# Where the turned probabilities, the late key sums and the hidden layer norm stand in a two-layer cross-attention kernel

## The reference

```python
x = single_head_attention(x, ctx)                       # softmax over 361 context rows
for layer in (1, 2):
    h = layer_norm(x) * scale + offset
    q = h @ wq + bq; k = ctx @ wk + bk; v = ctx @ wv + bv          # heads of 128
    k = concat(k, bias_k); v = concat(v, bias_v)                   # one more key and value
    x = x + softmax(q k^T / sqrt(128)) v @ wo + bo
x = x + gelu(layer_norm(x) @ w_fc1 + b_fc1) @ w_fc2 + b_fc2
```

## Time and profile before

| | |
|---|---|
| median of three runs | 1750.81 us (1749.13 to 1752.08) |
| the profiled execution, own time | 1752.08 us |
| its span in the profile | 1750.2 us |
| PE busy | 1728.7 us |
| DVE busy | 1194.3 us |
| ACT busy | 751.4 us |
| POOL busy | 870.7 us |
| DMA queue, share of 16 engines | 33.2% |

### The profile page before, as it was taken

The page is one execution under the profiler, slowest core; times in us unless marked ns, Lnnn a source line. Parts: engine busy times, 40 slices in busy tenths (PEclk is TensorE's granted clock), DMA queues, the critical chain, the costliest instruction groups (busy, mean ns, idle before and its releaser), DMA issues.

```text
span 1750.2 us, 30234 instructions
## 1 busy us (share of the span) xinstructions
PE 1728.7 (99%) x10854; PEld 1679.7 (96%) x10854; DVE 1194.3 (68%) x2718; ACT 751.4 (43%) x1624; POOL 870.7 (50%) x727
## 2 busy tenths in 40 slices
PE   8999999999999999999999999999999999999999
PEld 5899999999998999999999999999999999999999
DVE  3667676766877766667876666668776676677675
ACT  3635334334544333335453343345443333444654
POOL 2674252454484452534882523555834535336754
PEclk9999999999999999999999999999999999999999
DMA  7732332223452232324342322334423233204332
GB/s 277 253 114 79 78 98 53 71 82 96 138 158 63 78 83 72 89 48 144 115 126 73 86 48 75 85 106 131 144 52 89 63 75 86 79 19 140 132 129 80
DMA packets 162784, 175.09 MB, mean 100 GB/s; under 512 B 99660, under 2 KB 115276, under 8 KB 162636
## 3 DMA queue, kind: packets, MB, share of 16 engines
q1 hardware_dynamic: 159388, 168.86, 33.2%
q10 hardware_dynamic: 3248, 4.30, 0.8%
HBM read 150.67 MB, written 5.14 MB: 89 GB/s over the span
## 4 chain that ended last, share of the span: by engine, by line
PE 92%; DVE 5%; ACT 1%; issue 1%; DMA 1%; SPq 0%; ACTq 0%; DVEq 0%
PE psum L819 29%; PE psum L820 29%; PE psum L821 29%; PE psum L1157 2%; PE psum L853 2%; DVE key_stage_late L1710 1%; DVE pT L1684 1%; DVE prob L1989 1%; DVE centred L1890 0%; DMA key_stage_late<-head_w_dram 0%; SPq L563 0%; PE psum L832 0%; DVE a_lo L1684 0%; ACT prob L1520 0%; DVE stats L1980 0%
## 5 line engine op out<-in xcount | busy, mean ns | idle before, releaser
L653 POOL TENSOR_TENSOR wbuf_hi<-stage,zero_col 128x512 fp32r<-128x512 f32 x256 | 272.5, 1065 | 673.9 <-PE psum L821 497.1
L708 POOL TENSOR_TENSOR wbuf_lo<-stage,wbuf_hi 128x512 fp32r<-128x512 f32 x256 | 336.8, 1316 | 20.1
L819 PE MATMUL psum<-pT,ctx_rows_hi 128*128 128x250 f32 (+1 forms) x1152 | 331.4, 288 | 5.9 <-DVE pT L1684 5.7
L820 PE MATMUL psum<-pT,ctx_rows_hi 128*128 128x250 f32 (+1 forms) x1152 | 331.1, 287 | 0.0
L821 PE MATMUL psum<-pT,ctx_rows_lo 128*128 128x250 f32 (+1 forms) x1152 | 330.4, 287 | 0.0
L819 PE MATMUL psum<-ctxT_hi,a_hi 128*125 128x362 f32 (+1 forms) x832 | 277.8, 334 | 0.5
L821 PE MATMUL psum<-ctxT_hi,a_lo 128*125 128x362 f32 (+1 forms) x832 | 273.0, 328 | 0.0
L820 PE MATMUL psum<-ctxT_lo,a_hi 128*125 128x362 f32 (+1 forms) x832 | 272.8, 328 | 0.0
L819 PE MATMUL psum<-a_hi,wbuf_hi 128*128 128x400 f32 x720 | 252.7, 351 | 0.6 <-DVE xT L1905 0.6
L820 PE MATMUL psum<-a_lo,wbuf_hi 128*128 128x400 f32 x720 | 247.7, 344 | 0.0
L821 PE MATMUL psum<-a_hi,wbuf_lo 128*128 128x400 f32 x720 | 247.6, 344 | 0.0
(11 more groups left out here) (220 smaller groups left out, 3397.4 us busy)
## 6 DMA issues: line engine op xcount, KB each, us to landing
stage<-head_w_dram SPq DMA_DIRECT2D x256, 256.0 KB, 2.8
mlp_stage<-mlp_w_dram SPq DMA_DIRECT2D x32, 512.0 KB, 3.3
ctx_rows_in<-ctx_dram SPq DMA_DIRECT2D x20, 768.0 KB, 5.3
ctxT_in<-ctxT_dram SPq DMA_DIRECT2D x20, 724.0 KB, 5.4
p_b<-p_scratch SPq DMA_DIRECT2D x64, 200.0 KB, 3.6
sorted<-prob SPq DMA_DIRECT2D x256, 48.0 KB, 2.0
key_stage<-head_w_dram SPq DMA_DIRECT2D x22, 256.0 KB, 4.7
pT<-prob SPq DMA_DIRECT2D x96, 48.0 KB, 2.0
```

Source lines behind the costliest of these rows:

```text
L653: return nc.gpsimd.tensor_tensor(out, in_, zero_col[0:in_.shape[0], :].broadcast_to(tuple(in_.shape)), ALU.add)
L708: nc.gpsimd.tensor_tensor(lo, held, hi.bitcast(F32), ALU.subtract).then_inc(stage_free, 1)
L819: pe.matmul(out, a_h, x_hi, start=start, stop=False)
L820: pe.matmul(out, a_h, x_lo, start=False, stop=False)
```

## The change

Turning: `in_squares` keeps only the blocks with x = 0 (not the first two steps of units 2 and 4), with one held buffer. 16 blocks of a phase go in squares instead of 22, and 36 by PE instead of 30. The blocks that move are x = 1 of (1,1), (1,2), (2,2), (3,1), (3,2) and (4,2).

Late keys: all ten are in phase 0, two in each of the same five steps. The first ("a") stands ahead of `maxima(k, b, 1)` and the second ("b") at the end of the step. SP loads two behind each of the sorts of (0,1,0), (0,2,0), (0,3,0), and the others behind weights 8, 18, 20 and 21.

SP's reads of first rows: they stand behind all sorts of the same place, so those of heads 0 and 1 now stand behind the sort of (1, 1, 0).

DVE: an `o` piece at the head of place "a" (steps (1,3) and (3,3)) is added after `normalise` and not ahead of it. `hidden_centre` stands behind `normalise(k, b, 1)`, and the reciprocals of the variance are interleaved with `attended_lo`. In the single-head part two low parts of the context stand earlier.

PE: `hidden_mean` and `hidden_variance` stand behind `scores(k, b, 1)`. ACT: the four squares stand together behind `probs_hi(5, 1, 0)`. `PIECES`: v4 and v9 stand behind k7 and k12.

```diff
-    (2, 0, "b"): "q7 v2 v3 v4 o2 k7", ...
+    (2, 0, "b"): "q7 v2 v3 o2 k7 v4", ...
-    (4, 0, "b"): "q12 v7 v8 v9 o7 k12", ...
+    (4, 0, "b"): "q12 v7 v8 o7 k12 v9", ...
-LATE_KEYS_IN = 2
-LATE_KEYS_AT = [(0, 1), (0, 2), (0, 3), (1, 2), (1, 3)]
-FIRST_LATE_KEY_BEHIND = 9
-LATE_KEYS_BEHIND_SORTED = [(0, 2, 0), (0, 3, 0), (1, 0, 0), (1, 3, 0)]
+LATE_KEYS_AT = {(0, 1): "ab", (0, 2): "ab", (0, 3): "ab", (1, 2): "ab", (1, 3): "ab"}
+LATE_KEYS_BEHIND = {8: 1, 18: 1, 20: 1, 21: 1}
+LATE_KEYS_BEHIND_SORTED = {(0, 1, 0): 2, (0, 2, 0): 2, (0, 3, 0): 2}
 def in_squares(k, b, x):
-    return 0 < k + (x == 0) and k < len(UNITS) - 1 and not (k in LATE and b < 2) and not (x == 1 and b in (0, NB - 1))
-HELD = 2
+    return k < len(UNITS) - 1 and x == 0 and not (k in LATE and b < 2)
+HELD = 1
@@ SP
-                    reads = [h for h in VALUES if P0_READ_AT[h] == i and UNIT_OF[h] < LAST_UNIT]
                     for at in IN_SQUARES:
                         if SORTED_AT[at] == i:
-                            while reads and T_AT[LAST_BLOCK_OF[reads[0]]] < T_AT[at]:
-                                load_first_probs(ph, reads.pop(0))
                             sort_squares(ph, *at)
-                            if ph < LATE_KEYS_IN and at in LATE_KEYS_BEHIND_SORTED:
+                            for _ in range(LATE_KEYS_BEHIND_SORTED.get(at, 0) if ph == 0 else 0):
                                 load_late_key_weights(next(keys))
-                    for h in reads:
-                        load_first_probs(ph, h)
+                    for h in VALUES:
+                        if P0_READ_AT[h] == i and UNIT_OF[h] < LAST_UNIT:
+                            load_first_probs(ph, h)
@@ PE
                         scores(k, b, 0)
-                        if (k, b) == MEAN_IN:
-                            hidden_mean()
 ...
+                        scores(k, b, 1)
                         if (k, b) == VARIANCE_IN:
                             hidden_variance()
-                        scores(k, b, 1)
+                        if (k, b) == MEAN_IN:
+                            hidden_mean()
@@ ACT
-                        if STEPS[STEPS.index((k, b)) + 1:][:1] == [MEAN_IN]:
-                            hidden_square(ph, part)
 ...
                         probs_hi(k, b, 0)
+                        if (k, b) == MEAN_IN:
+                            hidden_squares(ph)
@@ DVE
-                        added_first = 1 if in_squares(k, b, 0) and pieces((k, b, "a"))[:1] and pieces((k, b, "a"))[0][0] == "o" else 0
-                        run_pieces((k, b, "a"), 0, added_first)
                         normalise(k, b, 0)
-                        run_pieces((k, b, "a"), added_first)
+                        run_pieces((k, b, "a"))
 ...
+                        if ph == 0 and "a" in LATE_KEYS_AT.get((k, b), ""):
+                            late_key_sums(next(keys))
                         maxima(k, b, 1)
+                        normalise(k, b, 1)
                         if (k, b) == MEAN_IN:
                             hidden_centre(ph)
                         if (k, b) == VARIANCE_IN:
-                            hidden_invert(ph, 0, DC - 1)
-                        normalise(k, b, 1)
-                        if before is not None:
+                            for part in range(DC - 1):
+                                attended_lo(*before, part, part + 1)
+                                hidden_invert(ph, part, part + 1)
+                            attended_lo(*before, DC - 1, DC)
+                        elif before is not None:
                             attended_lo(*before)
```

More of the change, by code:

```diff
@@ L90 @@
 KEYS = 7
-LATE_KEYS_IN = 2
-LATE_KEYS_AT = [(0, 1), (0, 2), (0, 3), (1, 2), (1, 3)]
-FIRST_LATE_KEY_BEHIND = 9
-LATE_KEYS_BEHIND_SORTED = [(0, 2, 0), (0, 3, 0), (1, 0, 0), (1, 3, 0)]
-KEYS_BEFORE = LAYERS * H - LATE_KEYS_IN * len(LATE_KEYS_AT)
+LATE_KEYS_AT = {(0, 1): "ab", (0, 2): "ab", (0, 3): "ab", (1, 2): "ab", (1, 3): "ab"}
+LATE_KEYS_BEHIND = {8: 1, 18: 1, 20: 1, 21: 1}
+LATE_KEYS_BEHIND_SORTED = {(0, 1, 0): 2, (0, 2, 0): 2, (0, 3, 0): 2}
+KEYS_BEFORE = LAYERS * H - len("".join(LATE_KEYS_AT.values()))
 PHASES = [(half, l) for l in range(LAYERS) for half in range(HALVES)]
@@ L427, in in_columns @@
             return ap.rearrange("p t (a j) -> p t a j", j=SQUARE)
-        held = [sorted0[:, :, :]] + [pT[:, 0:GROUPS, WIDE - RUN:WIDE].bitcast(F32)]
+        held = [sorted0[:, :, :]]
         def held_chunks(j):
@@ L558, in sort_squares @@
                     sp.wait_ge(p0_sent[x], 32 * n)
-                if x == 1:
-                    wait(sp, u_mm, ph * U_LAYER)
                 for a in range(GROUPS):
@@ L589, in _ @@
                 for i in range(early + 2 * (ph > 0), W_AT["v", H - 1]):
-                    reads = [h for h in VALUES if P0_READ_AT[h] == i and UNIT_OF[h] < LAST_UNIT]
                     for at in IN_SQUARES:
                         if SORTED_AT[at] == i:
-                            while reads and T_AT[LAST_BLOCK_OF[reads[0]]] < T_AT[at]:
-                                load_first_probs(ph, reads.pop(0))
                             sort_squares(ph, *at)
-                            if ph < LATE_KEYS_IN and at in LATE_KEYS_BEHIND_SORTED:
+                            for _ in range(LATE_KEYS_BEHIND_SORTED.get(at, 0) if ph == 0 else 0):
                                 load_late_key_weights(next(keys))
-                    for h in reads:
-                        load_first_probs(ph, h)
+                    for h in VALUES:
+                        if P0_READ_AT[h] == i and UNIT_OF[h] < LAST_UNIT:
+                            load_first_probs(ph, h)
                     load_weights(ph, i)
-                    if ph < LATE_KEYS_IN and i == FIRST_LATE_KEY_BEHIND:
-                        load_late_key_weights(next(keys))
+                    if ph == 0:
+                        for _ in range(LATE_KEYS_BEHIND.get(i, 0)):
+                            load_late_key_weights(next(keys))
                     if i == X_BEHIND:
@@ L1431, in norm_hi, with hidden_squares @@
                                              bias=norm_p[:, PARAMETERS[j], c, OFFSET_COL:OFFSET_COL + 1]).then_inc(n_hi, 1)
-            def hidden_square(ph, c):
-                act.wait_ge(hn_cen, ph * DC + c + 1)
-                nc.scalar.activation(x_held[:, c, :], centred[:, c, :], ACT.Square).then_inc(hn_sq, 1)
+            def hidden_squares(ph):
+                for c in range(DC):
+                    act.wait_ge(hn_cen, ph * DC + c + 1)
+                    nc.scalar.activation(x_held[:, c, :], centred[:, c, :], ACT.Square).then_inc(hn_sq, 1)
             def hidden_roots(ph):
@@ L1482, in queries_hi @@
                 def queries_hi(h):
-                    if ph < LATE_KEYS_IN and h == ASIDE[0]:
-                        act.wait_ge(kw_sum, KEYS_BEFORE + (ph + 1) * len(LATE_KEYS_AT))
+                    if ph == 0 and h == ASIDE[0]:
+                        act.wait_ge(kw_sum, LAYERS * H)
                     nc.scalar.activation(made_queries(h)[0], made("q", h), ACT.Identity, bias=bias_of(BQ, h))\
@@ L1801, in single_head @@
                 turned_lo(0)
+                ctx_columns_lo(1, 0)
                 queries1_lo(1)
@@ L1805, in single_head @@
                 probs0_lo(2)
-                ctx_columns_lo(1, 0)
+                ctx_columns_lo(1, 1)
                 queries1_lo(2)
@@ L1811, in single_head @@
                 probs0_lo(3)
-                ctx_columns_lo(1, 1)
                 queries1_lo(3)
@@ L1964, in add_output, with run_pieces @@
                         add(columns(xT[:, m, :]), made("o", h, m), columns(xT[:, m, :]), l, m, h == 0).then_inc(y_done, 1)
-                def run_pieces(place, start=0, stop=None):
-                    for kind, h in pieces(place)[start:stop]:
+                def run_pieces(place):
+                    for kind, h in pieces(place):
                         {"q": queries_lo, "k": through_keys_lo, "v": values_lo, "o": add_output}[kind](h)
@@ L2088, in layer @@
                             hidden_scale(ph, 0, 1)
-                    if ph < LATE_KEYS_IN and (k, b) in LATE_KEYS_AT:
+                    if ph == 0 and "b" in LATE_KEYS_AT.get((k, b), ""):
                         late_key_sums(next(keys))
-                    if ph == LATE_KEYS_IN - 1 and (k, b) == (3, 2):
+                    if ph == 0 and (k, b) == (3, 2):
                         key_parts(1)
```

## The result

The changed kernel takes 1770.01 us in the median of 4 runs (1768.51 to 1772.52), beside 1749.97 (1749.13 to 1752.08, 4 runs) for the kernel before on the same chip: a ratio of 1.0114, 95% interval [1.0097, 1.0132], or +20.0 us. The forecast was +10.6, 1761.5 with a range of 1754 to 1769. The direction was right, the size was half, and the time lies above the range.

What follows compares the result with a forecast made beforehand. PE, busy for 1728.7 of 1750.2 us, was taken to bound the kernel. The terms 7.7 - 7.6 + 1.2 + 3.2 + 4.6 + 1.5 gave +10.6 us, so 1761.5, with a range of 1754 to 1769.

Steps and rivals of the forecast that it cites:

- six blocks a phase turned by PE: PE, all phases: 24 blocks at 0.32 us each, all on the path, +7.7 us; bounds 6 and 19.
- late keys leave phase 1: First two units of phase 1: its 7.6 us over phase 2 go, -7.6 us; far bound 0.
- late keys double in phase 0: DVE in phase 0: added key sums fall partly into idle time, +1.2 us; bounds 0 and 4.3.
- late reads: SP's first-row reads behind the sorts: DVE stands still 6.3 us in (1,1), PE loses 0.8 a phase, +3.2 us.
- adds behind `normalise`: Steps (1,3) and (3,3): adds begin 2.65 us after o1, 0.65 over the reserve; seven steps, +4.6 us.
- hidden norm, with the reciprocals: Unit 5: mean no longer fills a wait, variance waits 0.1 each, +1.5 us; interleaved reciprocals cost nothing.
- earlier context parts: DVE in the single-head part: reordering within idle time of over 1 us, costs nothing.
- v4 and v9: Their new place costs nothing; k7 still waits for a bank that was filled five before.
- 19 us of the mean duration: Upper bound for the turned blocks: 0.27 us a transpose, the mean duration of such a row.
- The key term: Phase 0: the sums' move was called better than by count because POOL has no context rows to split there.
- the key sums repay all: Rival: (0,3)'s key lands earlier in phase 0, its stalls go, waits hide; -2 us, 1749; chance 0.09.
- A deeper stall: Rival: v0's row lands at 4.8 us, or gaps in unit 1 of phase 0 lower the clock; 1766 to 1769; chance 0.18.

Runs made afterwards that it cites:

- e1: The kernel before with only the six blocks a phase with x = 1 turned by PE: 1758.76 us, ratio 1.0037.
- e5: The kernel before with only all ten late key sums moved to phase 0: 1744.41 us, ratio 0.9965.
- e4: The kernel before with only the two low parts of the context columns earlier in DVE's single-head part: 1753.19 us, ratio 1.0016.
- e8: The kernel before with late keys in phase 0, v4 and v9 behind k7 and k12, one key load behind a later sort: 1742.85 us, ratio 0.9957.
- e7: The kernel before with only the hidden mean behind the scores and the centring behind the scaling: 1752.65 us, ratio 1.0010.
- e13: The kernel before with all late keys in phase 0 and o1 and o6 added behind `normalise`: 1755.40 us, ratio 1.0028.
- e2: The kernel before with only SP's reads of the first rows of heads 0 and 1 behind the sorts: 1764.27 us, ratio 1.0069.
- e3: The kernel before with only o1 and o6 added behind `normalise`: 1763.54 us, ratio 1.0065.
- e6: The kernel before with the whole hidden norm as changed (mean, variance, centring, squares together, reciprocals interleaved): 1755.47 us, ratio 1.0034.

## Why the prediction was too low

By its own steps (the column of the changed kernel is the sum of the steps over four phases in its profile):

| term | forecast | steps in the changed kernel | runs |
|---|---|---|---|
| six blocks a phase turned by PE | +7.7 | +7.7 | +6.5 (e1) |
| late keys leave phase 1 | -7.6 | -6.4 | -6.1 for both key terms (e5) |
| late keys double in phase 0 | +1.2 | -0.3 | |
| late reads | +3.2 | +5.6 | 4.9 undone, 12.1 alone |
| adds behind `normalise` | +4.6 | +5.7 | 4.0 undone, 11.4 alone |
| hidden norm, with the reciprocals | +1.5 | +5.3 | 4.4 undone, 5.6 alone |
| earlier context parts | 0 | +2.2 | +2.8 (e4) |
| v4 and v9 | 0 | -1.3 | in e8 |
| sum | +10.6 | +18.5 | +20.0 |

The spans differ by 16.7 only, because the profiled execution of the kernel before had the clock at half between 109 and 116 us and that of the changed kernel had no such stretch at all; this is worth some 2 us.

**Right.** The price of a turned block, read as a distance, was right to 0.01 us, and the 19 us of the mean duration or the 28 by the figure of the Trainium skill (VectorE: DVE Perf Modes, section The three transpose paths) would have been far off. The keys went out of phase 1 as said. The adds begin 2.67 us behind o1, as worked out, and cost 0.5 to 0.6 in the undisturbed phases. One premise of the key term did not hold: in phase 0 POOL has no context rows to split, but its weight splits collide with the sums too. Of the sum in (1,3) of phase 0 one instruction took 1.37 us before and one takes 1.36 in the changed kernel (224.97). The term did not suffer by it. The rival "the key sums repay all" was wrong: phase 0 hardly changed. "A deeper stall", 1766 to 1769, was nearest in size and had the wrong reason: the clock fell less often than before, and v0's row landed in 3.6, 3.9 and 4.2 us in phases 0, 1 and 2, not in 4.8.

**Wrong: "the interleaved reciprocals, the earlier context parts in the single-head part and the place of v4 and v9 cost nothing".** This was argued from DVE's idle time before those places. DVE idled there for ACT (1.30 us ahead of the low part of the probabilities), and the step that failed is that the moved part would take as long there as in its old place: POOL was busy in that idle time and had begun first, so the part took 4.65 us instead of 1.78. I had the same effect in the earlier trace rows (1.37 against 0.29) and used it for the keys alone. It is 2.8 of the missing 9.4. The reciprocals add about 2 more, and the order of v4 and v9 gives 1.3 back, though the forecast had k7 wait for its bank in either order.

**Mis-sized: the hidden norm, +1.5.** The place of the mean was priced well (+1.75 by e7, reckoned at 0.36 in three phases, 1.1). For the late squares only the variance's wait was counted, not where POOL's adds land: on DVE's scaling of the probabilities. 5.3 against 1.5.

**Mis-sized: SP's late reads, 0.8 a phase.** The chain was right in each link. The landing was too short: v0's row took 4.16 us and not the median of 3.6, so that DVE waited 6.94 instead of 6.3. The scaling took 0.55 instead of 0.42, and PE's step is 1.2 longer instead of 0.5. With 0.1 at `attend` it measured 1.3 a phase (1.9 in phase 0, 1.1 in phase 1).

**Interactions.** The terms were worked out for the whole, and there their steps agree with what the undone parts gave back. Alone, two of them cost twice as much. For the adds the rows of e13 show the cause, an alignment of DVE with POOL and a fall of the clock. For the reads e2 shows two waits instead of one, and a third at the late key sum of phase 1; by the steps these are 10.5 of 12.1.

## What to carry to other kernels

Before an instruction is moved into idle time of DVE, look at what POOL does in that time and which of the two begins first: here the same instruction took 0.42 or 1.28, 1.78 or 4.65 us, and PE waited for it. A part that moves one engine's work by a microsecond must be followed to where the next engine's work lands, not only to the first consumer. And where a change bundles gains and losses, run the gaining part alone: the keys' move with the order of v4 and v9 (e8) is 0.43% faster than the kernel before, while the whole is 1.14% slower.

## What the runs showed of the hardware that was not expected

The stretches at half clock lie at different places from one execution to the next, and their number differs, for the same kernel. Of the 76 timed executions of the kernel before, (1 - mean granted clock) x time averages 3.2 us. For the changed kernel it is 1.8 (5 executions), for e5 2.0 (6), and for e3 and e13, with waits of about 2 us in (1,3) or (3,3), 5.9 (6) and 5.4 (12); each clock is given to 0.001, which is 1.75 us, so only such means say anything. So more waiting doesn't mean more time at half clock: of these kernels the changed one has the most PE idle in its profile (33.3 us) and lost least. Nor does one gap tell it. The prediction held against a fall of the clock that the gap of 1.84 us at `attend` of (0,3) in phase 0 had brought none. At the same place the clock fell behind 2.16 us in the profile of e5 and 2.25 in that of e6, and did not behind 2.38 in that of e13 and 2.68 in that of e1.
